# All batches resident in SBUF and an unrolled front with the normalisation on ScalarE, in an SSM and mixture-of-experts kernel

## The reference

```python
xn = (u - mean) / sqrt(var + 1e-5)
h[t] = lam * h[t-1] + xn[t] @ B_w.T          # 64 states, a scan over the tokens of a batch
y = h @ C_w.T + D * xn
aff = (xn @ waff.T) / (norm(xn) * norm(waff) + 1e-9)     # 8 experts
cap = clip(floor(512 * sigmoid(mean(aff) - threshold)), 4, 512)
mask[e] = (argmax(aff) == e) & (rank of aff[:, :, e] within its batch < cap)
for e in range(8):
    moe += gelu((xn * mask[e]) @ W1[e] + b1[e]) @ W2[e] + b2[e]     # W1: 256 x 1024, W2: 1024 x 256
```

## Time and profile before

| | us |
|---|---|
| median of 3 runs (lowest, highest) | 754.84 (752.55, 758.89) |
| the profiled execution | 750.57 |
| its span in the profile | 748.8 |
| TensorE busy | 593.1 (79%) |
| VectorE busy | 568.1 (76%) |
| GpSimd busy | 459.5 (61%) |
| ScalarE busy | 321.2 (43%) |

### The profile page before, as it was taken

How to read it: one execution, slowest core, us unless ns; L and a number is a source line. 1 busy time by engine, 2 the same in 40 slices (tenths; PEclk the granted TensorE clock), 3 DMA queues, 4 the chain that set the end, 5 groups by cost and what they waited for, 6 DMA issues and landing times.

```text
span 748.8 us, 16312 instructions
## 1 busy us (share of the span) xinstructions
PE 593.1 (79%) x4593; PEld 494.0 (66%) x4594; DVE 568.1 (76%) x1068; ACT 321.2 (43%) x586; POOL 459.5 (61%) x526
## 2 busy tenths in 40 slices
PE   2726555654654754699999999999999999999995
PEld 1423333433323643588889888988898898888884
DVE  3798987988898897769776676667667666766763
ACT  2733543453340966343443344344334434433440
POOL 0453742653570054638888887787778778777743
PEclk9956656656665786889999999999999999999998
DMA  7476656566122000002222222121221211211100
GB/s 243 170 245 213 222 170 216 179 208 214 60 86 70 2 1 30 27 17 67 63 71 77 70 71 62 57 73 57 71 64 46 70 59 49 72 58 46 50 26 5
DMA packets 48682, 68.36 MB, mean 91 GB/s; under 512 B 7159, under 2 KB 40208, under 8 KB 48656
## 3 DMA queue, kind: packets, MB, share of 16 engines
q1 hardware_dynamic: 33744, 37.61, 15.6%
q0 software_dynamic: 11232, 25.20, 11.0%
q10 hardware_dynamic: 3680, 5.24, 2.0%
HBM read 46.25 MB, written 27.26 MB: 98 GB/s over the span
## 4 chain that ended last, share of the span: by engine, by line
PE 61%; DVE 26%; issue 5%; ACT 3%; DMA 1%; POOL 1%; SPq 1%; DVEq 1%; ACTq 0%; POOLq 0%
DVE wlo L892 6%; DVE work L948 6%; PE ps_bu L762 5%; PE ps_bu L764 5%; PE ps_bu L763 5%; PE ps_t L743 4%; PE ps_t L744 4%; PE ps_t L745 4%; PE ps_y L744 4%; PE ps_y L743 4%; PE ps_y L745 4%; PE ps_num L764 4%; PE ps_num L763 4%; PE ps_num L762 4%; PE ps_y L647 2%
## 5 line engine op out<-in xcount | busy, mean ns | idle before, releaser
L339 POOL TENSOR_TENSOR work<-work,d_bc 128x1024 f32<-128x1024 f32 x16 | 52.0, 3252 | 97.8 <-DVE work L948 89.1
L422 POOL DMA_INDIRECT out<-work,idx_b x78 | 96.7, 1240 | 19.1 <-issue 14.1
L570 ACT ACTIVATE ring<-ps_t,b1t,inv_in 128x256 f32<-128x256 f32 x156 | 79.4, 560 | 56.3 <-PE ps_t L745 45.2
L432 POOL DMA_INDIRECT work<-base_rows,idx_b x78 | 88.9, 1140 | 18.0 <-issue 15.2
L398 POOL DMA_INDIRECT ring<-xn_rows,idx_x x78 | 82.8, 1061 | 27.1 <-issue 19.9
L762 PE MATMUL ps_bu<-whi,ring 128*128 x320 | 88.4, 276 | 5.6 <-DVE ring L1219 5.6
L570 ACT ACTIVATE ring<-ps_y,b1t,inv_in 128x256 f32<-128x256 f32 x156 | 79.5, 560 | 22.0 <-PE ps_y L745 21.4
L763 PE MATMUL ps_bu<-wlo,ring 128*128 x320 | 88.5, 276 | 0.0
L764 PE MATMUL ps_bu<-whi,ring 128*128 x320 | 88.4, 276 | 0.0
L743 PE MATMUL ps_t<-ring,whi 128*128 128x256 f16 x312 | 85.9, 275 | 1.6 <-DVE ring L1205 1.4
L744 PE MATMUL ps_t<-ring,whi 128*128 128x256 f16 x312 | 85.8, 275 | 0.0
(11 more groups left out here) (297 smaller groups left out, 1432.5 us busy)
## 6 DMA issues: line engine op xcount, KB each, us to landing
ring<-L_ffn_W SPq DMA_DIRECT2D x12, 1024.0 KB, 5.6
xn_rows<-work SPq DMA_DIRECT2D x16, 512.0 KB, 3.8
base_rows<-work SPq DMA_DIRECT2D x16, 512.0 KB, 3.1
work<-L_attn_u SPq DMA_DIRECT2D x14, 512.0 KB, 4.3
ring<-L_ffn_W ACTq DMA_DIRECT2D x4, 1024.0 KB, 9.4
ring<-xn_rows,idx_x POOLq DMA_INDIRECT x78
work<-base_rows,idx_b POOLq DMA_INDIRECT x78
out<-work,idx_b POOLq DMA_INDIRECT x78, 2.7
```

Source lines behind the costliest of these rows:

```text
L339: g.tensor_tensor(dxn, xnb[h], d_bc[:].rearrange("p (a d) -> p a d", a=1).to_broadcast([P, Q, D]), ALU.mult).then_inc(s["dx_ok"], 1)
L422: g.indirect_dma_start(out=out_rows, out_offset=bass.IndirectOffsetOnAxis(ap=idx_b[:, 2 * ro + h:2 * ro + h + 1], axis=0), in_=og[ro % 2][ ...
L432: g.indirect_dma_start(out=bg[rb % 2][:, h * D:(h + 1) * D], out_offset=None, in_=base_dram, in_offset=bass.IndirectOffsetOnAxis(ap=idx_b[ ...
L570: ins = a.activation(h32[:, c * W:(c + 1) * W], ps_h[qt][:, c % CQ * W:(c % CQ + 1) * W], ACT.Gelu, bias=b1t[:, bass.ds(e * C + c, 1)], sc ...
```

## The change

- **Batches.** All 16 batches lie in SBUF at once, in one tensor `area`; as they leave, the split weights take their places (`home_free` is the wait for such a place). The front is unrolled. A batch lies as (p q): partition p holds tokens 4p to 4p+3, so the transposes write every fourth PSUM column, and `every_q` reads the states with a stride of four.
- **Normalisation** is four ScalarE operations a batch, xn = rstd x u - mean x rstd, with the factors as pointers (`normal`). VectorE keeps the moments and the 1/std.
- **Routing rows** go through the scan with the states (72 rows; their factor is zero) and are transposed by TensorE into ps_num (`states_out`). No copy on ScalarE and no trip through DRAM is left for them.
- **y** of every batch goes to ps_y, and one VectorE operation adds it (`add_y`).
- **Weights.** Only units 0 to 3 are split in the front (`lows`, `highs`, `sums`, `scales` give the batch behind which each piece stands). Units 4 to 11 are loaded and split in the routing, and 12 to 15 (W2 of experts 4 to 7) in the first four steps of the loop, through `raw_late`. The sums of a pair of units go to DRAM and come back broadcast (`bound`), in place of the TensorE's turning. The low half of a W1 unit reads its source with a stride of eight elements.
- **Zero rows** are f32 matmuls from the raw W2 unit (`zero_row`), copied by ScalarE and added to c_bc by GpSimd, before the first gather. Before, they were f16 matmuls and VectorE added them, between the first tiles.
- **Search.** High parts and weight sums stand between the search's rounds (`first_half`, `second_half`).
- **Places.** In each of four quarters 16 pairs of short operations and one long one (`places`), where two-dimensional operations on half tiles stood. The places of the kept tokens (`kept_places`, 64 operations and a TensorE product) now stand ahead of the loop.

The core of the diff:

```diff
+        def home_free(eng, n):
+            e, w = unit(n)
+            if w == 0 and e < 4:
+                xn_stored(eng, e)
+                eng.wait_ge(s["dx_ok"], 2 * (2 * e + 2))
+                eng.wait_ge(s["xt_ok"], K * (2 * e + 2))
+            elif w == 0:
+                eng.wait_ge(base_out[e - 4], 16)
+            elif e < 4:
+                eng.wait_ge(base_out[e + 4], 16)
+            else:
+                eng.wait_ge(s["kept_inv"], 1)
...
+            def bound(r):
+                sp.wait_ge(s["wsum_ok"], 2 * r + 2)
+                sp.dma_start(bound_rows[r:r + 1, :].rearrange("a (p w) -> (a p) w", w=2), wsum[:, 2 * r:2 * r + 2]).then_inc(s["bound_out"], 16)
+                sp.wait_ge(s["bound_out"], 16 * r + 16)
+                wait(sp, s["wscale_ok"], r - 1)
+                if r >= 3:
+                    sp.wait_ge(s["dx_ok"], 2 * B)
+                sp.dma_start(wall(r), bound_rows[r:r + 1, :].rearrange("a c -> (a c)").partition_broadcast(P)).then_inc(s["bound_in"], 16)
...
+            bound(2)
+            base_store(5)
+            raw_in(6)
...
+            raw_in(10)
+            raw_in(11)
+            bound(4)
+            raw_in(12)
+            raw_in(13)
+            bound(5)
+            raw_in(14)
+            raw_in(15)
+            bound(6)
+            bound(7)
+            sp.wait_ge(s["mask_ok"], 1)
+            for n in range(EARLY, UNITS):
+                wait(sp, s["wlo_ok"], n if n > EARLY else 0)
+                sp.dma_start(raw_late, w2_v[unit(n)[0]]).then_inc(s["w_late"], 16)
...
+            for e in range(E):
+                pool.wait_ge(s["g_out"], e + 1)
+                wait(pool, s["c_ok"], e)
+                g.tensor_tensor(c_bc[:, :], c_bc[:, :], g_bc[:, e * D:(e + 1) * D], ALU.add).then_inc(s["c_ok"], 1)
...
+            def normal(b):
+                act.wait_ge(s["rstd_ok"], b // 2 + 1)
+                for q in range(Q):
+                    t = b * Q + q
+                    last = a.activation(xn_(b)[:, q * D:(q + 1) * D], xu_(b)[:, q * D:(q + 1) * D], ACT.Identity,
+                                        scale=rstd[:, t:t + 1], bias=nmr[:, t:t + 1])
+                last.then_inc(s["xn_ok"], 1)
+            def turned(b):
+                for k in range(K):
+                    act.wait_ge(s["xt_ok"], K * b + k + 1)
+                    wait(act, s["bu_ok"], b - 1)
+                    a.copy(xnt[b % 2][:, k, :], ps_t[:, k * S:(k + 1) * S]).then_inc(s["xt_out"], 1)
...
+            deviation(0)
+            normal(0)
+            deviation(1)
+            sums = {4: 0, 5: 1, 7: 2, 8: 3, 12: 4, 13: 5}
+            highs = {8: 0, 9: 1, 11: 2, 12: 3}
+            for b in range(B):
+                if b + 1 < B:
+                    normal(b + 1)
+                turned(b)
...
+            def first_half(n):
+                if n == 8:
+                    high_part(6, raw[2])
+                    high_part(7, raw[3])
+            def second_half(n):
+                if n == 0:
+                    weight_sum(8)
+                    weight_sum(9)
+                if n == 6:
+                    high_part(8, raw[0])
+                    high_part(9, raw[1])
+                if n == 10:
+                    weight_sum(10)
+                    weight_sum(11)
             act.wait_ge(s["key_hi_ok"], 1)
-            find(key_hi, 14, s["hi_found"])
+            find(key_hi, 14, s["hi_found"], first_half)
             act.wait_ge(s["key_lo_ok"], 1)
-            find(key_hi, 16, s["lo_found"])
+            find(key_hi, 16, s["lo_found"], second_half)
+            high_part(10, raw[2])
+            high_part(11, raw[3])
+            for e in range(4):
+                zero_row(e)
+            for n in range(EARLY, UNITS):
+                weight_sum(n)
+            for e in range(4, E):
+                zero_row(e)
...
+                if isinstance(j, int) and j < LATE:
+                    act.wait_ge(s["w_late"], 16 * (j + 1))
+                    high_part(EARLY + j, raw_late)
...
+            def states_out(b):
+                pe.wait_ge(s["scan_ok"], b + 1)
+                for q in range(Q):
+                    last = t.transpose(ps_num[:, q * P + b * E:q * P + (b + 1) * E], every_q(hs[b % 2][N:NE, :], q),
+                                       ident[N:NE, N:NE])
+                last.then_inc(s["num_ok"], 1)
+                wait(pe, s["base_ok"], b)
+                for q in range(Q):
+                    last = t.matmul(ps_y[:, q * D:(q + 1) * D], every_q(hs[b % 2][0:N, :], q), ct[0:N, :],
+                                    start=True, stop=True)
+                last.then_inc(s["y_ok"], 1)
...
+            def zero_row(e):
+                n = E + e
+                pe.wait_ge(w_in[n % 4], 16 * (n // 4 + 1))
...
+                wait(pe, s["g_out"], e // 2 * 2 - 2)
+                for c in range(C):
+                    last = t.matmul(ps_y[:, e % 4 * D:(e % 4 + 1) * D], gelu_b[:, e * C + c:e * C + c + 1].to_broadcast([P, P]),
+                                    raw[n % 4][:, c * D:(c + 1) * D], start=(c == 0), stop=(c == C - 1))
+                last.then_inc(s["g_pe"], 1)
+            for e in range(6):
+                zero_row(e)
+            pe.wait_ge(s["kept_ok"], 1)
...
+            for e in range(6, E):
+                zero_row(e)
...
+            def add_y(b):
+                dve.wait_ge(s["y_ok"], b + 1)
+                dve.wait_ge(s["dx_ok"], 2 * b + 2)
+                v.tensor_tensor(xu_(b), ps_y[:, :], xu_(b), ALU.add).then_inc(s["base_ok"], 1)
...
+                if w == 0:
+                    v.scalar_tensor_tensor(out=low(e, w, 0, UW).rearrange("p (c f) -> p c f", c=C),
+                                           in0=src.rearrange("p (f c) -> p c f", c=C), scalar=scale_w[:, n:n + 1],
+                                           in1=high(e, w, 0, UW).rearrange("p (c f) -> p c f", c=C),
+                                           op0=ALU.mult, op1=ALU.subtract).then_inc(s["wlo_ok"], 1)
...
-                        for q in range(Q):
-                            tt = h * Q + q
-                            ins = v.tensor_scalar(xnb[h][:, q, :], xb[n][:, q, :], mv[pr][:, 2 * tt:2 * tt + 1],
-                                                  rstd[pr][:, tt:tt + 1], ALU.subtract, ALU.mult)
-                        ins.then_inc(s["xn_ok"], 1)
-                    if not (first and pr == 0):
-                        low_part(pair, pr, 0)
-                        low_part(pair, pr, 1)
...
+            lows = {9: 0, 10: 1, 13: 2, 14: 3}
+            scales = {7: 0, 10: 1, 15: 2}
+            for b in range(B):
+                states(b)
+                if b + 4 < B:
+                    last = moments(b + 4)
+                    if b % 2 == 1:
+                        link(last)
+                        variance((b + 3) // 2)
+                if b % 2 == 0 and 2 <= b <= 12:
+                    rstd_of((b + 2) // 2)
+                if b > 0:
+                    add_y(b - 1)
+                if b in scales:
+                    weight_scales(scales[b])
+                if b in lows:
+                    low_part(lows[b], raw[lows[b] % 4])
...
+            def places(qt):
+                for t_ in range(qt * TQ, (qt + 1) * TQ):
+                    v.tensor_scalar(lo16[:, t_, :], iota16[:, :], lo_f[:, t_:t_ + 1], None, ALU.is_equal)
+                    last = v.tensor_scalar(v1[:, t_, :], iota16[:, 0:NS], hi_f[:, t_:t_ + 1], float(S * (t_ % B + 1)),
+                                           ALU.is_equal, ALU.mult)
+                link(last)
+                wait(dve, s["plane_used"], qt - 1)
+                v.tensor_scalar(v0[qt % 2], v1[:, qt * TQ:(qt + 1) * TQ, :], 0.5, pcolq[:, qt:qt + 1],
+                                ALU.is_ge, ALU.mult).then_inc(s["planes_ok"], 1)
+            assert TQ == B
+            places(0)
+            places(1)
+            low_part(6, raw[2])
+            low_part(7, raw[3])
+            places(2)
             dve.wait_ge(s["hi_found"], 1)
             v.tensor_scalar(search[:, 4:5], search[:, 0:1], -1.0, None, ALU.mult)
             link(v.tensor_scalar(key_hi, key_hi, search[:, 0:1], 2.0 ** 17, ALU.add, ALU.mult))
             v.memset(search[:, 0:1], -(2.0 ** 15 - 0.5))
             v.tensor_tensor(key_hi, key_hi, low_half, ALU.add).then_inc(s["key_lo_ok"], 1)
...
+            def kept_places():
...
+                link(v.tensor_tensor(te(gap), te(ps_bu0[:, 0:S]), et(oh), ALU.mult))
+                link(v.tensor_reduce(mtok, te(gap), AX.X, ALU.add))
+                for t_ in range(T):
+                    last = v.tensor_scalar(v1[:, t_, :], iota16[:, 0:NS], hi_f[:, t_:t_ + 1], mtok[:, t_:t_ + 1],
+                                           ALU.is_equal, ALU.mult)
+                last.then_inc(s["slots_ok"], 1)
                 dve.wait_ge(s["kept_inv"], 1)
-                v.tensor_copy(mask_slot, ps_num[:, 0:NS]).then_inc(s["mask_ok"], 1)
-            def masked_sum():
```

(10 more changed lines are left out.)

1168 lines of the change are left out of this document (520 added, 648 removed).

## The result

The changed kernel took 826.82 us (median of 4 runs, 821.73 to 828.39), the kernel before beside it 756.87 (4 runs, 752.55 to 762.49): a ratio of 1.091, 95% interval 1.082 to 1.100. The forecast was 779 with a range of 747 to 812. The sign was right, the size was not: 24 us slower was forecast, 70 were measured.

The account below looks back on a forecast made before the run. The front was taken as bound by a ring over VectorE and TensorE, the loop by TensorE. Front 179 + routing 155 + loop start 5 + loop 425.8 + output 9.2 = 774 us of span, predicted as 779, range 747 to 812.

Parts of the forecast that it names:

- The ring: Front: scan, statistics, addition of y, y, Bu (product with B_w) and next scan wait in a circle; 10.3 us a turn.
- The eleven turns: Front: the scan-to-scan intervals after the first, forecast as eleven of 10.3 us each.
- ScalarE "has room": Front: ScalarE can take over the normalisation, some 2.0 us a batch.
- The first product: Start of the front: first product with B_w (Bu) done at 23.5 us, as fewer parameters stand ahead.
- From the front to the first tile: Routing: 155 us from the front's end to the first expert tile (ends 137 and 172), 64.8 before.
- The second key: Routing: VectorE's key for the search's second half, ready 57 us after the front's end; ScalarE waits 14 us.
- that step: Routing behind the search: ScalarE's splits and zero-row copies, then zero rows 4 and 5 on TensorE; ends at 107.4 us.
- A: Rival, front: TensorE stays at full clock, front ends at 160, total 760 us, the same time; chance 0.2.
- B: Rival, front and routing: full-clock front and routing at its short ends, total 742 us, faster; chance 0.09.
- C: Rival, front: strided access on TensorE doubles transposes and loads of y's stationary rows, total 805 us; chance 0.16.
- The slow clock throughout: Front: TensorE slow in every turn, front 207 us for 179, total 807; told under C, no chance of its own.
- D: Rival, front: batches' stores hold back a weight load or scale, one stop of 5 to 8 us, 785; 0.55 with forecast.

Follow-up runs that it names:

- e3: Changed kernel with sixteen unread f16 matmuls added on TensorE in each turn from the fourth on, where it waits for the addition; span 801.3 us.
- e1: Changed kernel with VectorE's addition of the previous batch's y put ahead of the scan; median 800.18 us, ratio to the kernel before 1.070.
- e6: Changed kernel with additions ahead of scans as in e1, and ScalarE's copies ahead of the next normalisation; median 782.15 us, ratio to before 1.050.
- e9: Changed kernel with the orders of e6, e7, e8, plus ScalarE's square root and TensorE's late-parameter matmuls moved later; median 745.31 us, ratio to before 0.996.
- e11: e9 with the square norms and their root moved to the end of the thirteenth batch's step; span 746.4 us, ratio to the kernel before 0.986.
- e8: Changed kernel with kept tokens' transposes ahead of the last four zero rows, low halves 10 and 11 ahead of kept places; span 795.5 us, ratio 1.070.
- e7: Changed kernel with low halves 6 and 7 put behind the second key on VectorE; span 811.8 us.
- e5: Changed kernel run again unedited, on the chip of the experiments; median 817.75 us, ratio to the kernel before 1.098.
- e4: Changed kernel with every stride of four on TensorE made contiguous, output not the reference's; median 812.81 us against 817.75 unedited.

## Why the prediction was wrong

**The ring: right in its links, wrong in its clock.** The prediction gave 8.9 us at full clock and 12.2 at half, and chose 10.3 because the new ring "has dense work more often". The eleven turns took 12.1 on average. The step that failed is that choice. The new ring has an idle stretch of 2.3 to 2.7 us in every one of them, ahead of y, and behind it y takes 2.7 to 3.8 us and Bu 3.1 to 3.7, against 2.2 and 1.9 at full clock; a busier engine is not the same as one without gaps. e3 shows it by filling the gap (8.7 us in a plain turn), e1 and e6 by taking it away (10.1, then 6.3 to 7.5). Nine of the eleven turns average 11.6 us, which is some 12 of the 52.7; the other two, of 14.3 us, add 8 and belong to the next paragraph.

**ScalarE "has room": true of its busy time, false of its order.** The prediction gave 3 us for weight work that does not fit in VectorE's gap, and nothing for ScalarE, whose queue has high halves, sums and waiting square roots ahead of the normalisation and the copies. From 32 to 212 us six of these square roots wait for VectorE's moments, 49.3 us in all. Two of the eleven turns took 14.3 us, and the last three 9.1, 15.6 and 8.3 in place of 8 each. One such turn with what lies ahead of it (timeline):

```profile
151.56 5.88 DVE L910 SCALAR_TENSOR_TENSOR area<-ring,scale_w,area 128x2048 f16<-128x2048 f32 x1
153.88 5.72 POOL L398 TENSOR_TENSOR area<-area,work 128x1024 f32<-128x1024 f32 x1
...
160.78 0.21 ACT L498 ACTIVATE rstd<-work 128x8 f32<-128x8 f32 x1 [8.46 <-DVE work L869]
160.93 4.00 ACT L527 ACTIVATE area<-ring,scale_w 128x2048 f16<-128x2048 f32 x1
...
164.84 2.06 ACT L504 ACTIVATE area<-area,work,rstd 128x256 f32<-128x256 f32 x4
166.80 1.04 ACT L512 COPY work<-ps_t 128x512 f32<-128x512 f32 x2
...
167.90 3.69 PE L688 MATMUL ps_bu<-work,bwt 128*72 128x512 f32 x4 [3.21 <-ACT work L512]
```

The low half and GpSimd's addition lie side by side and take 5.9 and 5.7 us, where 3.9 and 2.3 are usual; that they slow each other is a reading, no run separates them. The moments stand behind the low half, and ScalarE's square root waits 8.5 us for them. Then ScalarE has a high half of 4 us ahead of the normalisation (2.1) and the copies (1.0), so that TensorE, done with y, waits 3.2 us for them and runs Bu at half clock. The turn of 15.6 us has the same form with another root, that of the norms:

```profile
187.53 0.26 ACT L558 ACTIVATE work<-work 128x64 f32<-128x64 f32 x1 [10.73 <-DVE work L965]
```

Behind it come a weight sum, the normalisation and the copies, and Bu waits 6.1 us for them. In the orders of e9 this turn took 15.5 us; e11 moves the root, and it falls to 6.1.

**The start.** The first product was put at 23.5 because "fewer parameters stand ahead". TensorE has two small matmuls on late parameters ahead of it and waits for these until 26.6: 8.8 us. The order of the rows showed it, and the prediction did not use it. Moved in e9, among other orders, the first scan comes at 23.2.

**From the front to the first tile: 167 for 155.** Mostly the right chain, with errors of both signs. The second key was ready 64.3 us in, not 57: the scales of units 6 and 7 came at 31.7, not 28, and three quarters of places took over a microsecond more each. The wait forecast at 14 us was 16.2:

```profile
276.97 0.72 ACT L587 ACTIVATE work<-work,search 128x512 f16<-128x512 f32 x1 [16.19 <-DVE work L1117]
```

The end of this stretch, from the chain of waits:

```profile
318.32 9.88 PE ps_y L748 x32
328.20 0.48 PE ps_bu L757 x4
...
330.48 11.12 DVE area L1168 x53
...
344.14 4.10 PE ps_bu L761 x64
...
348.42 2.35 DVE area L915
...
350.79 4.84 DMA ring<-L_ffn_W
...
355.68 10.01 PE ps_y L748 x32
```

Two terms were mis-sized. A pair of zero rows is 16 matmuls and was counted as eight; each of the two pairs takes 9.9 to 10.0 us, at a mean clock of 0.72 and 0.71, where 6.8 stood for half clock. (The terms of that step, 93.5, 4.0, 0.9 and 6.8, add up to 105.2, and 107.4 was written.) The 64 operations for the kept tokens' places take two columns as pointer operands, where the row used has an integer operation of 64 columns, and cost 0.21 us each, not the 0.11 of the earlier trace rows: 13.6 us, not 7.0. The loads behind them then came 3 to 4 us sooner than forecast. That this chain is dearer than the wait in the search, e8 (21.1 us) and e7 (2.6 us) show.

**The loop: 5 us were forecast for its start, 0.3 are there.** The late weight halves cost nothing visible. By e5 the term was 5 us too large; the profile shows 7.1 us more than forecast only because of the 11.8 us in seven long tiles, which e5 does not have.

**The strides.** VectorE and ScalarE pay, and TensorE pays a little where nothing waits for it. Low halves read with a step of eight against plain ones (columns: busy us, mean ns, idle before):

```profile
L910 DVE SCALAR_TENSOR_TENSOR area<-ring,scale_w,area 128x2048 f16<-128x2048 f32 x8 | 33.0, 4151 | 0.1
...
L915 DVE SCALAR_TENSOR_TENSOR area<-ring,scale_w,area 128x2048 f16<-128x2048 f32 x4 | 9.2, 2347 | 2.5 <-ACT area L531 2.5
```

The typical strided one takes 3.9 us, 1.6 more than plain; 3.8 was forecast from the one strided row of before. ScalarE's high half of a W1 unit, read with the same step, takes 4.0 us where a W2 unit takes 2.0; the forecast had 2.0 to 3.4. And eight transposes that write every fourth PSUM column at half clock, 0.23 us each, as the 16 of the earlier trace rows took 0.24:

```profile
107.20 1.84 PE L680 MATMUL ps_t<-ident,area 128*128 128x128 f32 x8
```

The Trainium skill, "Advanced Engine Details and Errata", Memory Cachelines, warns of strided PSUM access for matmuls; in f32 transposes with a step of four, e4 finds no cost (1.04 and 1.92 us for eight, with and without). What it says of SBUF fits VectorE's reads (3.9 against 2.3 us) and the loads of y's rows (304 against 182 ns).

**The rivals.** A and B asked for full clock in the front, and it came only in turns whose gap was gone or filled (e1, e3, e6). C gave 805, among the nearest to the measured total, by a mechanism that costs this kernel nothing; that is luck. The slow clock throughout, which the same paragraph put at 207 for the front and 807 in all, came nearest to what happened (y and Bu slow in every turn, a front of 212.6), and it was counted as the edge of the range. D is not seen: from 32 to 212 us no engine's wait in the profile ends with a DMA.

## What to carry to other kernels

When each batch hangs on the one before through several in-order queues, write out every ring with the place of each operation in its queue, since the busy share of an engine says nothing about that, and take away all rings of one length together (14.5 and 0 us alone, 33 together). An idle stretch of two or three microseconds on TensorE has to be priced with the half clock behind it, as long as TensorE is in the ring; here it cost up to 3.3 us in y and Bu of one turn. A large change that is 9% slower may be so by its orders alone: the six reorderings of e9 gave back 72 us here and brought the kernel level with the one before.
